# FFN products of the first and the last job ahead of their gates, fills up to the first value product, and the last store in two

## What is computed

```python
x = x + 0.5 * _L0_ffn_ref(_layernorm(x), W, b, R, A, B)
x = x + _L0_attn_ref(_layernorm(x), W_kv, g_kv, W_kdec, W_vdec, W_q, W_qdec, W_krope, W_qrope, W_o)
x = x + 0.5 * _L0_ffn_ref(_layernorm(x), W, b, R, A, B)
# FFN: x W^T + b + sum over the top 2 of 8 experts of gate_e * B_e (A_e x), rank 16 each
# attention: 16 heads, 16 content + 32 rotary dims, v of 16, latent k/v of 64, latent q of 128, causal softmax
```

## Time and profile before

| | |
|---|---|
| median of 3 runs | 1935.3 us (1933.92 to 1936.35) |
| profiled execution | 1934.23 us, span 1932.5 us |
| TensorE busy | 1879.5 us (97%) |
| VectorE, ScalarE, GpSimd busy | 1437.6, 1019.7, 854.0 us |
| granted TensorE clock, mean | 0.988 |
| HBM traffic | 178.99 MB read, 126.22 MB written |

### The profile page before, as it was taken

One profiled execution on the slowest core, in us unless ns is written; L12 is line 12 of the kernel. 1 busy time (PEld: TensorE's weight loads), 2 busy tenths in 40 slices (PEclk: granted clock), 3 DMA queues, 4 the chain that ended last, 5 costly groups with the idle time before them and its releaser, 6 DMA issues.

```text
span 1932.5 us, 33217 instructions
## 1 busy us (share of the span) xinstructions
PE 1879.5 (97%) x11308; PEld 1333.4 (69%) x11308; DVE 1437.6 (74%) x4570; ACT 1019.7 (53%) x2125; POOL 854.0 (44%) x912
## 2 busy tenths in 40 slices
PE   8779999999999999999999999999999999999998
PEld 7546666667767777667767767677777777777656
DVE  5667787777787778877777787777787787777643
ACT  3435565555554655555555455545655555555452
POOL 3455554443553544554453555435454444532112
PEclk9889999999999999999999999999999999999999
DMA  3685676677666467755666665665776566675621
GB/s 105 193 194 145 169 187 171 156 176 177 161 159 168 133 178 191 181 135 164 176 169 170 173 180 162 163 159 158 187 178 178 130 168 172 162 179 135 128 51 44
DMA packets 169768, 307.51 MB, mean 159 GB/s; under 512 B 15104, under 2 KB 33792, under 8 KB 169600
## 3 DMA queue, kind: packets, MB, share of 16 engines
q1 hardware_dynamic: 169600, 305.40, 62.5%
HBM read 178.99 MB, written 126.22 MB: 158 GB/s over the span
## 4 chain that ended last, share of the span: by engine, by line
PE 84%; DVE 7%; DMA 4%; ACT 2%; issue 2%; POOL 1%; SPq 1%; POOLq 0%; DVEq 0%
PE st_b L751 14%; PE mx_b L783 14%; PE st_b L753 12%; PE o_b L771 12%; PE tp_b L819 6%; PE wj_b L706 5%; PE tp_b L816 4%; PE wj_b L693 3%; PE wj_b L675 3%; PE wj_b L708 2%; PE wj_b L686 2%; DMA st<-k_scratch 2%; PE wj_b L715 1%; PE wj_b L721 1%; DVE mx_b L974 1%
## 5 line engine op out<-in xcount | busy, mean ns | idle before, releaser
L860 ACT ACTIVATE probs<-st_b 128x512 f32<-128x512 f32 (+3 forms) x1536 | 703.2, 490 | 571.3 <-PE st_b L753 528.0
L974 DVE CUSTOM_DVE_ANT_0 mx_b<-mx_b,tri 128x256 f32<-128x256 f32 (+3 forms) x1024 | 510.8, 515 | 104.5 <-PE mx_b L783 100.3
L751 PE MATMUL st_b<-st 97*128 97x512 f32 (+2 forms) x1536 | 577.3, 381 | 7.3 <-ACT probs L860 5.7
L783 PE MATMUL mx_b<-st 96*128 96x256 f32 (+2 forms) x1536 | 550.6, 402 | 22.0 <-DVE mx_s L974 12.4
L753 PE MATMUL st_b<-st,k_st 96*128 96x512 f32 (+2 forms) x1536 | 523.0, 345 | 0.0
L977 DVE TENSOR_REDUCE mx_s<-mx_b 128x1 f32<-128x512 f32 (+1 forms) x512 | 334.5, 653 | 135.4 <-PE mx_b L783 129.3
L1175 POOL TENSOR_SCALAR_AFFINE_SELECT probs<-probs 128x512 f32<-128x512 f32 x256 | 169.6, 668 | 553.8 <-ACT probs L860 553.5
L783 PEld LDWEIGHTS mx_b<-st 96*128 96x128 f32 x1536 | 282.2, 192 | 167.3 <-issue 68.7
L751 PEld LDWEIGHTS st_b<-st 97*128 97x128 f32 x1536 | 291.1, 190 | 121.4 <-issue 52.9
L753 PEld LDWEIGHTS st_b<-st,k_st 96*128 96x128 f32 x1536 | 293.3, 191 | 28.8 <-issue 9.1
L771 PE MATMUL o_b<-probs,v_s 128*17 128x512 f32 (+3 forms) x3328 | 286.7, 466 | 0.7 <-POOL probs L1175 0.7
(11 more groups left out here) (198 smaller groups left out, 2322.1 us busy)
## 6 DMA issues: line engine op xcount, KB each, us to landing
st<-q_scratch SPq DMA_DIRECT2D x128, 384.0 KB, 5.7
st<-k_scratch SPq DMA_DIRECT2D x128, 384.0 KB, 8.6
k_st<-k_scratch SPq DMA_DIRECT2D x128, 384.0 KB, 9.6
q_scratch<-hi_t SPq DMA_DIRECT2D x32, 768.0 KB, 3.8
q_scratch<-lo_t SPq DMA_DIRECT2D x32, 768.0 KB, 5.1
k_scratch<-hi_t SPq DMA_DIRECT2D x30, 768.0 KB, 6.3
k_scratch<-lo_t SPq DMA_DIRECT2D x30, 768.0 KB, 4.9
ao_scratch<-o_f SPq DMA_DIRECT2D x252, 32.0 KB, 1.7
```

What stands on the lines that cost most here:

```text
L751: nc.tensor.matmul(dst, k1_st[u][0:SHIFT + 1, a, P * j:P * j + P], q_st[u][0:SHIFT + 1, a, q0:q0 + w], start=True, stop=False)
L783: nc.tensor.matmul(mx_b[:, m % 2, 0:w], q_st[u][0:SHIFT, a, P * i:P * i + P], k1_st[u][0:SHIFT, a, k0:k0 + w], start=True, stop=True).then ...
L860: nc.scalar.activation(probs[:, a, PLACE[s]:PLACE[s] + n], st_b[:, a % 2, HALF - n:HALF], ACT.Exp, scale=SCALE).then_inc(exp_done, 1)
L974: nc.vector.tensor_tensor_reduce(src, src, tri[:, HALF - n:HALF], 1.0, NEG, ALU.add, ALU.max, dst).then_inc(mx_done, 1)
```

## The change

1. In jobs 0 and 31 the eight products of xt with W become a step of their own ("ahead") before gated_tr, into two banks that are free at that time: one each of mx_b and st_b for job 0, the two of wj_b for job 31. y0 and y1 of these jobs keep the two products with bt per bank.
2. The fills: D goes from 67 to 90, d (at the end) from 43 to 30, and a third kind, e, writes to o_b between job 1's last product and the first value product: 33 of them.
3. Job 31's store of 512 KB becomes two of 256 KB, each behind the add of its bank.
4. The strings of all five engines are written anew up to the fourteenth group of heads; from there on they are as before, but for the fills at the end.

```diff
+AHEAD = (0, NJ - 1)
+def job_steps(n):
+    out = list(job_mm(n))
+    if n in AHEAD:
+        out.insert(out.index("gated_tr"), "ahead")
+    return out
...
 ORDER = {
     "PE": (
-        "DDDDDDDDDDDDDDDDDDDDDDDDDDDDDDDJJJJDDDDDDDDDDPDPDPDPDDjjjjJDJJjDjjJJDJJPjjPjPJjPDPDPDDDDDDDDDDDDDDPDPJPJ"
+        "DDDDDDDDDDDDDDDDDDDDDDDDDDDDDDDJJJJJPDPDPDPDDjjjjJDJJDDDDDDDDDDDDDDDDDjDJJjJJPjPJPDDDDPDPDPDDDDDDDDDDDDD"
...
+        "e": [("warm", 2)] * order_of("PE").count("e"),
...
         def wj_of(n, name):
+            if n in AHEAD and name in ("y0", "y1"):
+                return (lanes[0].banks if n else [mx_b[:, 0, :], st_b[:, 0, :]])[int(name[1])]
             return lanes[LANE[n]].banks[bank_use(n, name) % 2]
...
                 elif name == "x_store":
...
+                    if n == NJ - 1:
+                        for part in range(2):
+                            sp.wait_ge(own.wj_free, bank_use(n, f"y{part}") + 1)
+                            sp.dma_start(out_g[k][:, 2 * part:2 * part + 2, :],
+                                         own.xa[:, 2 * part:2 * part + 2, :]).then_inc(own.stored, 16)
+                        continue
...
+                if name == "ahead":
+                    if n:
+                        pe.wait_ge(lanes[0].wj_free, sum(len(job_mm(i)) for i in range(NJ) if not LANE[i]))
+                    for tk in range(GT):
+                        c = D * (tk % 2)
+                        for kk in range(KD):
+                            nc.tensor.matmul(wj_of(n, f"y{tk // 2}")[:, c:c + D], xt[:, tk, P * kk:P * kk + P],
+                                             w1_s[:, kk, 0:D], start=(tk % 2 == 0 and kk == 0), stop=False)
+                    return
...
-                        for kk in range(KD):
+                        for kk in range(KD if n not in AHEAD else 0):
                             nc.tensor.matmul(dst, xt[:, tk, P * kk:P * kk + P], w1_s[:, kk, 0:D], start=(kk == 0),
                                              stop=False)
-                        last = nc.tensor.matmul(dst, ght[:, P * tk:P * tk + P], bt_s[:, :], start=False, stop=True)
+                        last = nc.tensor.matmul(dst, ght[:, P * tk:P * tk + P], bt_s[:, :], start=False,
+                                                stop=(n not in AHEAD or tt == 1))
...
-                    if g:
+                    if g == 1:
                         pe.wait_ge(mx_done, NM * QUADS)
-                    nc.tensor.matmul(mx_b[:, 1, 0:P], ident[:, :], ident[:, :], start=True, stop=True)
+                    elif g == 2:
+                        pe.wait_ge(lanes[1].wj_free, len(job_mm(1)))
+                    nc.tensor.matmul((o_b[:, 0, 0:P] if g == 2 else mx_b[:, 1, 0:P]), ident[:, :], ident[:, :],
+                                     start=True, stop=True)
```

More of the change, by code:

```diff
@@ L218 @@
[L218 to L219 removed]
+        "JwJJJJjjjJjwwJJJjJJJJJJjjjjjjJjJjJJjJjJJjJJjjjJJLJjJRLLLJJjjJJJJJJJJJJjjJLJJJMMJLMMRMMJMMJMMjMMMLLMMMfnM"
+        "MLMMMMMMMMLMMMMMMMMMMMMMMMMLMMLMMMMMfMMMMLMMnMMMMMLMMMMfMMLoMMnoooMMMMLMMMMMMMMLMMJMMMLJMMMJMJJMMJMMMMMM"
+        "fLMMnMMLMMJMMJMMoMMoMoMoJJMMfJMMnMJMJMJMJMJMMJLMMJMMLoMMoooMMMJMMJMMJJJMMMJJMMLMMMMMfnLMMJMMJMMJMMoMMoJM"
```

177 lines of the change are left out of this document (108 added, 69 removed).

## The result

| | before | changed |
|---|---|---|
| median of four runs each | 1935.2 us | 1944.3 us (1943.1 to 1944.8) |
| ratio, 95% interval | | 1.0050 (1.0035 to 1.0065) |
| span of the profiled execution | 1932.5 us | 1942.2 us |
| mean granted TensorE clock | 0.988 | 0.989 |
| TensorE busy | 1879.5 us | 1892.8 us |

A forecast was written before the change was run, and what follows sets the result against it. TensorE was taken to bound the middle, so only the two ends could gain: end -4.1 and head -2.5 make -6.6, from a median of 1935.3 to 1928.7 us. The range was 1923.5 to 1935.0.

The forecast's parts named there:

- The end: Job 31: eight products ahead of the gated transpose save 3.4 us, the store in two halves 0.7; sum -4.1.
- The head, first paragraph: Start of the head: job 0's y1 ends near 29.3 us, most of 3.4 is given back, unit 1 some 2 earlier.
- Second paragraph: Head, second half of q and k: loads land at 112.0 us (bound 114.9), maxima resume 5.8 us later than before.
- D's deciding point: Rival on late loads in the head: slower, 1940.9 us, decided from a landing at 119.1 us; chance 0.08.
- Third paragraph: Head from 112.0 us: VectorE sets the pace with 25.5 us of work, and the mark comes at 147.0.
- the fold: VectorE's step closing the stretch of second-half maxima in the head: forecast at 137.5 us, practically the time of before.
- the mark: Head's end, first score of the first group needing the second shift row: from 154.88 to 147.0 us, -7.9.
- rival C: Clock falls to half among the head's maxima, TensorE 3.4 us late: -3.2 in all, 1932.1 us; chance 0.27.
- B's full clock: Rival: fills keep the head's clock up, no half clock at 144 to 150 us: -10.6, 1924.7 us; chance 0.12.
- Behind the mark I expect no difference: Middle of the kernel after the head: no gain or loss, its 19 us of idle time being spread over it.
- A new wait of over 1 us between 160 and 800 us: Sign that the forecast is wrong: a new wait of over a microsecond in that part of the middle.
- The 5.4 us of work not yet done at the mark: Head: two pieces, job 2's qc, six maxima and a turn still undone, taken off the -7.9 to leave -2.5.

The follow-up runs named there:

- e4_noe: The changed kernel without its 33 fills of kind e: 1948.5 us, ratio 1.0061.
- e16_best: The kernel before with the new end, 32 fills of kind e in the head, and ScalarE's fills of ones behind the twelfth exponential: 1928.4 us, ratio 0.9980.
- e9_job0: The kernel before with the new end and job 0's eight products ahead of its gates in place of ten fills: 1931.3 us, ratio 0.9986.
- e8_clock: The changed kernel with eleven more fills, one ahead of each pair of maxima between first value product and second turn: 1943.3 us, ratio 1.0057.
- e18_spots: The changed kernel with VectorE's steps moved: job 3's gate steps up together, job 7's power and normalization ahead of maxima: 1941.3 us, ratio 1.0047.
- e19_gates: The kernel before with the new end, 32 fills of kind e, and two maxima ahead of four gate steps of job 4: 1921.8 us, ratio 0.9952.
- e12_port: The kernel before with the new end and an extra GpSimd product beside the normalization of jobs 3 to 28: 1934.4 us, ratio 1.0006.

## Why the prediction was wrong

**The end**, "Sum of the end: -3.4 - 0.7 = -4.1": right in mechanism and size, 4.2 in the changed kernel, whether counted from the gated transpose or from job 31's first output projection, 3.7 in e4_noe, 3.1 in e16_best and 4.2 in the rest.

**The head, first paragraph** (y1 at 29.3 to unit 1): right, every time within a microsecond, and so was its judgement that most of the 3.4 us is given back. By e9_job0 all of it is.

**Second paragraph**, "the loads go out at 102.6 to 103.9" and "the queue is clear this time, so I take 8.1: 112.0". The last load landed at 116.3, above the bound of 114.9 and under D's deciding point of 119.1. Unit 3's last difference ended at 100.5 for 98.7. Its store took 3.7 us to land, as forecast. Then the loads stood another 1.7 us on the queue behind the first shift's store, whose turn came at 104.8 for 101.5; and the last of them landed 9.0 us after its issue, 8.1 reckoned. Part of this was the execution: in the five other traces with these strings the turn comes at 103.1 to 103.9 and the maxima resume at 114.6 to 115.0. The runs with the loads ahead moved the landing by 1 us against these, without a gain; what all 4.3 us cost they do not show.

**Third paragraph**, "from 112.0 VectorE sets the pace". This is the step of the head that failed. The forecast took VectorE's durations up to the fold, 25.5 us, as the length of the stretch. They were rightly counted (25.6 in the trace), but the stretch took 30.9, as long as before's 31.0; with the late landing that puts the fold 9.7 us late and the mark 8.7. The forecast's reading of before was wrong already: "busy 27 of 31 us" adds up durations that overlap in the pipeline. VectorE was busy 22.7 of 31.0, and the earlier trace rows themselves show 8.5 and 2.6 us of idle time ahead of its reduces and maxima (some of it before the stretch begins). TensorE was the busier engine in both (26.5 and 27.6 us), and with two banks each waits for the other in turn, so that VectorE's work is not the length even at full clock (28.9 in e8_clock). And the clock fell to half in it, as rival C said: C had +3.4, and the growth from the first score to 166 us is 1.3 to 6.8. B's full clock did not come. C had 0.27; its chance should have been the larger one, since before showed half clock in the same stretch.

**"Behind the mark I expect no difference"**. This is the other step that failed. Head and end alone would have made the kernel 1.9 us slower (6.1 - 4.2); the 7.8 behind the mark make it 9.7, and 5.0 of them are the three places named here. The new strings were read for which steps come when on one engine, never for what runs beside them on another: 4.2 us at 219 and 3.9 at 525, against 3 saved at 303. Both came back in every run with these strings that left the two places alone: 4.2 to 5.5 us for the first, 2.4 to 4.0 for the second. The profile of before had shown the mechanism, at 303, and no rival spoke of it. "A new wait of over 1 us between 160 and 800 us" stands among the signs of being wrong, and one came (2.09, beside the 1.8 in three parts under a microsecond each); only its cause was missing.

The 5.4 us of work not yet done at the mark were right (5.3 by the traces).

What stays open: the 2.8 us lost behind the mark besides these three places, part of it where the strings are the same; what the 4.3 us of late landing cost; and how an order would have to look in which the maxima of the second half take less than 29 us. More banks for the maxima, or all the head's waits taken away together, were not tried.

## What to carry to other kernels

When an order is rewritten, read it across engines as well as along them: for each VectorE step with two SBUF inputs or a tensor_scalar, look what GpSimd runs at that time, and keep the long GpSimd operations off the steps that TensorE waits for. Moving VectorE's short steps past a maximum or two was enough at two places (219 us in e18_spots, 303 in e19_gates) and failed at a third; moving the long operation drags along whatever other engines have queued for it. Waits of 1.8 and 2.1 us on a full TensorE cost 4.2 and 3.9 here, because half clock followed. Where two engines hand a pair of banks to each other, take the length of the stretch from a trace that has it, not from the busier engine's sum of durations.

## What was not expected of the hardware

- VectorE's 128 x 32 operations took up to 1.31 us beside a GpSimd rotation for 0.18 alone, and a 128 x 256 tensor_scalar up to 1.42 (1.48 in e12_port) for 0.41; reduces were not touched. The held-up step ended 0.05 (tensor_tensor) or 0.15 us (tensor_scalar) behind the GpSimd operation beside it.
- The same strings had between 10.2 and 23.9 us of half clock in one stretch of 45 us from one execution to the next, worth 5.5 us.
- An 8 KB store issued right behind two pairs of 384 KB loads took 8.3 us until its reader could be issued, 2.3 with nothing ahead. The Trainium skill (DMA: Bandwidth & Descriptors, on rings and completion order) says that each ring is consumed in order; the trace agrees, the store landing at 113.7 us, 0.2 behind the last load.
